# Turning one normalised copy of the tokens instead of two in an attention and feed-forward block

## The reference

```python
xn = _layernorm(x, axis=-1)
x = x + attn(xn, norm_w, Wq, Wkv, Wo, q_gamma, k_gamma) + ffn(xn, W1, b1, W2, b2, scale)
# in attn:
h = xn * rsqrt(mean(xn**2) + eps) * norm_w            # RMS norm over the layer norm
q, k, v = h @ Wq, split(h @ Wkv, 2)                   # 16 heads of 64
q = q / max(norm(q), 1e-12) * (q_gamma + 1) * 8       # each head of each token; k likewise
sim = tanh(q @ k.T / 50) * 50 / 8
out = softmax(sim) @ v @ Wo
```

## Time and profile before

| | |
|---|---|
| median of 3 runs | 1115.67 us (1115.66 to 1117.9) |
| the profiled execution | 1117.53 us |
| its span, first to last instruction | 1115.5 us |
| mean granted TensorE clock | 0.995 |
| busy: PE, PEld, DVE, ACT, POOL | 94%, 75%, 84%, 93%, 77% |
| chain that ended last | PE 49%, ACT 23%, DVE 18%, issue 8%, POOL 0% |
| DMA | 77 GB/s mean |

### The profile page before, as it was taken

How to read it: one execution, slowest core, us unless ns; L and a number is a source line. 1 busy time by engine, 2 the same in 40 slices (tenths; PEclk the granted TensorE clock), 3 DMA queues, 4 the chain that set the end, 5 groups by cost and what they waited for, 6 DMA issues and landing times.

```text
span 1115.5 us, 33883 instructions
## 1 busy us (share of the span) xinstructions
PE 1045.9 (94%) x12873; PEld 835.4 (75%) x12873; DVE 931.7 (84%) x2185; ACT 1034.0 (93%) x1543; POOL 854.0 (77%) x784
## 2 busy tenths in 40 slices
PE   3789999999999999999999999999999999999987
PEld 2557787777787777787777777777778777778776
DVE  4888898888898888889888889888889888889872
ACT  3599999999999999999999999999999999999996
POOL 5577787778788878778778778778778778778663
PEclk9899999999999999999999999999999999999999
DMA  4143343354343344443334444444335344344441
GB/s 149 40 82 68 80 85 69 73 87 73 80 81 73 74 82 76 79 80 77 77 74 79 80 80 78 73 77 80 78 79 82 69 77 87 74 79 77 70 91 30
DMA packets 310743, 86.45 MB, mean 77 GB/s; under 512 B 282036, under 2 KB 309816, under 8 KB 310584
## 3 DMA queue, kind: packets, MB, share of 16 engines
q1 hardware_dynamic: 310584, 84.30, 39.8%
HBM read 12.13 MB, written 4.19 MB: 15 GB/s over the span
## 4 chain that ended last, share of the span: by engine, by line
PE 49%; ACT 23%; DVE 18%; issue 8%; POOL 0%; ACTq 0%; POOLq 0%
PE ps_scores L492 11%; ACT probs L582 6%; ACT clamped L575 6%; PE ps_y L542 6%; PE ps_aux L467 6%; DVE qk L770 6%; PE ps_aux L426 5%; PE ps_o L520 4%; ACT L619 4%; DVE norm L685 3%; PE ps_aux L428 3%; PE ps_aux L427 3%; ACT hid L619 3%; PE ps_y L540 3%; PE ps_o L522 3%
## 5 line engine op out<-in xcount | busy, mean ns | idle before, releaser
L937 POOL TENSOR_TENSOR probs_lo<-probs 128x1024 f16<-128x1024 f32 x256 | 485.1, 1895 | 216.3 <-ACT probs L582 214.1
L575 ACT ACTIVATE clamped<-ps_scores 128x1024 f32<-128x1024 f32 x256 | 265.7, 1038 | 34.6 <-PE ps_scores L492 28.8
L582 ACT ACTIVATE probs<-clamped 128x1024 f32<-128x1024 f32 x256 | 273.3, 1067 | 2.2 <-PE ps_o L522 0.7
L520 PEld LDWEIGHTS ps_o<-v_hi,probs 128*128 128x128 bf16 x2048 | 183.9, 98 | 60.6 <-issue 58.1
L520 PE MATMUL ps_o<-v_hi,probs 128*128 128x65 bf16 x2048 | 213.8, 195 | 5.2 <-DVE newton_r L698 1.7
L492 PE MATMUL ps_scores<-heads_T 64*128 64x256 f16 x3072 | 212.8, 271 | 4.3 <-ACT clamped L575 4.2
L426 PE MATMUL ps_aux<-w_hi,xhT_hi 128*128 128x512 f32 x384 | 179.6, 468 | 38.7 <-DVE qk L770 29.1
L521 PE MATMUL ps_o<-v_lo,probs 128*128 128x64 bf16 x2048 | 211.8, 192 | 0.0
L522 PE MATMUL ps_o<-v_hi,probs_lo 128*128 128x65 bf16 x2048 | 211.4, 193 | 0.0
L521 PEld LDWEIGHTS ps_o<-v_lo,probs 128*128 128x128 bf16 x2048 | 187.3, 99 | 0.0
L522 PEld LDWEIGHTS ps_o<-v_hi,probs_lo 128*128 128x128 f16 x2048 | 187.3, 97 | 0.0
(11 more groups left out here) (80 smaller groups left out, 1927.1 us busy)
## 6 DMA issues: line engine op xcount, KB each, us to landing
heads_T<-halves SPq DMA_TRANSPOSE x512, 2.5
x_in<-in_L_attn_tokens_dram SPq DMA_DIRECT2D x32, 128.0 KB, 2.4
x_res<-in_L_attn_tokens_dram SPq DMA_DIRECT2D x32, 128.0 KB, 2.3
out_dram<-y_sb SPq DMA_DIRECT2D x32, 128.0 KB, 2.5
sel_raw<-xn SPq DMA_DIRECT2D x192, 4.0 KB
qk<-in_L_attn_Wkv_dram SPq DMA_DIRECT2D x2, 512.0 KB, 5.3
qk<-in_L_attn_Wq_dram SPq DMA_DIRECT2D x1, 512.0 KB, 3.7
qk<-in_L_ffn_W_dram SPq DMA_DIRECT2D x2, 256.0 KB
```

Of the source, the lines that this page charges most:

```text
L520: pe.matmul(full, hi[:, col], v_hi[:, par, u, h], start=(u == 0), stop=False)
L575: nc.scalar.activation(clamped[:].rearrange("p j n -> p (j n)"), ps_scores[:].rearrange("p j n -> p (j n)"), ACT.Tanh).then_inc(clamp_done, 1)
L582: nc.scalar.activation(probs[:, pair % RING].rearrange("p j n -> p (j n)"), clamped[:].rearrange("p j n -> p (j n)"), ACT.Exp, bias=LIFT, ...
L937: g.tensor_tensor(probs_lo[:, buf].rearrange("p j n -> p (j n)"), probs[:, buf].rearrange("p j n -> p (j n)"), probs[:, buf].rearrange("p ...
```

## The change

Only `xn` is made and turned. `xhT_hi`, `xhT_lo` and `xnT` are now all made from the turned `xn`. The RMS factor (one number per token) is applied where values leave PSUM, in `v_hi` and in `v_lo`; for queries and keys it goes into the floor under the norm, which is now one number per token and tile. The variance sums move from GpSimd to VectorE, which also divides them (`inv_eps`, `var_eps[:, 1]`); GpSimd keeps the power and makes the floor. The core of the diff:

```diff
-                    for t in range(TT):
-                        pe.transpose(bank[:, t * P:(t + 1) * P], xh[:, t], ident[:])
-                    for t in range(TT):
-                        ins = pe.transpose(bank[:, seq + t * P:seq + (t + 1) * P], xn[:, par, t], ident[:])
+                        ins = pe.transpose(bank[:, t * P:(t + 1) * P], xn[:, par, t], ident[:])
...
+                if kind == "v" and k == 0:
+                    act.wait_ge(rstd_made, b + 1)
...
-                    nc.scalar.copy(v_hi[:, par, t, 8 * c:8 * c + 8, 0:DH],
-                                   bank.rearrange("p (h d) -> p h d", d=DH)).then_inc(v_hi_made, 1)
+                    nc.scalar.activation(v_hi[:, par, t, 8 * c:8 * c + 8, 0:DH],
+                                         bank.rearrange("p (h d) -> p h d", d=DH), ACT.Copy,
+                                         scale=rstd[:, b % 4, 1, t:t + 1]).then_inc(v_hi_made, 1)
...
+                dve.wait_ge(meanvar_made, 2 * b + 2)
+                wait(dve, floor_made, b)
+                v.tensor_scalar(var_eps[:, 0], mean_var[:, :, 1], LN_EPS, None, ALU.add).then_inc(vareps_made, 1)
+                v.tensor_scalar(ms_eps[:], mean_var[:, :, 1], 1.0 + RMS_EPS, RMS_EPS * LN_EPS,
+                                ALU.mult, ALU.add).then_inc(vareps_made, 1)
+                dve.wait_ge(vareps_made, 2 * b + 2)
+                v.reciprocal(inv_eps[:], var_eps[:, 0]).then_inc(inveps_made, 1)
+                dve.wait_ge(inveps_made, b + 1)
+                v.tensor_tensor(var_eps[:, 1], ms_eps[:], inv_eps[:], ALU.mult).then_inc(ratio_made, 1)
...
-                    v.tensor_scalar(minus_half_norm2, norm2[:], NORM2_MIN, -0.5, ALU.max, ALU.mult)\
-                        .then_inc(seed_made, 1)
+                    dve.wait_ge(floor_made, b + 1)
+                    half_of = TT * HEADS
+                    for t in range(TT):
+                        part = slice(t * half_of, (t + 1) * half_of)
+                        v.tensor_scalar(minus_half_norm2[:, part], norm2[:, part], norm_floor[:, b % 4, t:t + 1], -0.5,
+                                        ALU.max, ALU.mult).then_inc(seed_made, 1)
...
-                    v.tensor_tensor(v_lo[:, par, t, 8 * c:8 * c + 8], bank.rearrange("p (h d) -> p h d", d=DH),
-                                    v_hi[:, par, t, 8 * c:8 * c + 8, 0:DH], ALU.subtract).then_inc(v_split, 1)
+                    v.scalar_tensor_tensor(v_lo[:, par, t, 8 * c:8 * c + 8], bank.rearrange("p (h d) -> p h d", d=DH),
+                                           rstd[:, b % 4, 1, t:t + 1], v_hi[:, par, t, 8 * c:8 * c + 8, 0:DH],
+                                           ALU.mult, ALU.subtract).then_inc(v_split, 1)
...
-                g.tensor_scalar(var_eps[:, 0], mean_var[:, :, 1], LN_EPS, None, ALU.add).then_inc(vareps_made, 1)
-                g.tensor_scalar(var_eps[:, 1], mean_var[:, :, 1], 1.0 + RMS_EPS, RMS_EPS * LN_EPS,
-                                ALU.mult, ALU.add).then_inc(vareps_made, 1)
-                pool.wait_ge(vareps_made, 2 * b + 2)
+                pool.wait_ge(ratio_made, b + 1)
...
+                g.tensor_scalar(norm_floor[:, b % 4], var_eps[:, 1], NORM2_MIN, None, ALU.mult).then_inc(floor_made, 1)
...
-                g.tensor_tensor(xh[:], x_mid[:], rstd[:, 1].unsqueeze(2).to_broadcast([P, TT, P]), ALU.mult)\
```

More of the change, by code:

```diff
@@ L194, in block_kernel @@
         var_eps = sb("var_eps", [P, 2, TT])
-        rstd = sb("rstd", [P, 2, TT])
+        ms_eps = sb("ms_eps", [P, TT])
+        inv_eps = sb("inv_eps", [P, TT])
+        rstd = sb("rstd", [P, 4, 2, TT])
+        norm_floor = sb("norm_floor", [P, 4, TT])
         xn = sb("xn", [P, 2, TT, P])
-        xh = sb("xh", [P, TT, P])
         x_mid = sb("x_mid", [P, TT, P])
@@ L267, in block_kernel @@
         seed_made = sem("seed_made")
+        ratio_made = sem("ratio_made")
+        inveps_made = sem("inveps_made")
+        floor_made = sem("floor_made")
         newton_step = sem("newton_step")
@@ L507, in values @@
                 if s == 3:
-                    wait(pe, seed_made, min(2 * (n + 2), 2 * batches))
+                    wait(pe, seed_made, min(3 * (n + 2), 3 * batches))
                 if s in (4, 5):
@@ L595, in aux @@
                 act.wait_ge(aux_filled[kind], PER_BATCH[kind] * b + k + 1)
+                if kind == "v" and k == 0:
+                    act.wait_ge(rstd_made, b + 1)
                 if kind == "xT":
                     nc.scalar.copy(xhT_hi[:, par], bank[:, 0:seq])
-                    nc.scalar.copy(xnT[:, b % 3], bank[:, seq:2 * seq]).then_inc(xnT_copied, 1)
+                    nc.scalar.copy(xnT[:, b % 3], bank[:, 0:seq]).then_inc(xnT_copied, 1)
                 elif kind == "q":
@@ L693, in seed @@
                     wait(dve, newton_step, 9 * b)
-                    v.tensor_scalar(minus_half_norm2, norm2[:], NORM2_MIN, -0.5, ALU.max, ALU.mult)\
-                        .then_inc(seed_made, 1)
+                    dve.wait_ge(floor_made, b + 1)
[4 more added lines that the diff above has]
+                                        ALU.max, ALU.mult).then_inc(seed_made, 1)
                 else:
-                    dve.wait_ge(seed_made, 2 * b + 1)
+                    dve.wait_ge(seed_made, 3 * b + 2)
                     v.tensor_scalar(newton_r[:].bitcast(I32), minus_half_norm2.bitcast(I32), -0.5, RSQRT_SEED,
@@ L704, in newton @@
                 if k == 0:
-                    dve.wait_ge(seed_made, 2 * b + 2)
+                    dve.wait_ge(seed_made, 3 * b + 3)
                 wait(dve, newton_step, 9 * b + k)
@@ L772, in aux @@
                 elif kind == "v":
+                    if k == 0:
+                        dve.wait_ge(rstd_made, b + 1)
                     dve.wait_ge(v_hi_made, 4 * b + k + 1)
                     t, c = k // 2, k % 2
-                    v.tensor_tensor(v_lo[:, par, t, 8 * c:8 * c + 8], bank.rearrange("p (h d) -> p h d", d=DH),
-                                    v_hi[:, par, t, 8 * c:8 * c + 8, 0:DH], ALU.subtract).then_inc(v_split, 1)
+                    v.scalar_tensor_tensor(v_lo[:, par, t, 8 * c:8 * c + 8], bank.rearrange("p (h d) -> p h d", d=DH),
+                                           rstd[:, b % 4, 1, t:t + 1], v_hi[:, par, t, 8 * c:8 * c + 8, 0:DH],
+                                           ALU.mult, ALU.subtract).then_inc(v_split, 1)
                 elif kind == "low":
@@ L856, in norm_rstd @@
                 b, _, _ = st.batch(ahead)
-                pool.wait_ge(meanvar_made, 2 * b + 2)
-                wait(pool, rstd_made, b)
-                g.tensor_scalar(var_eps[:, 0], mean_var[:, :, 1], LN_EPS, None, ALU.add).then_inc(vareps_made, 1)
-                g.tensor_scalar(var_eps[:, 1], mean_var[:, :, 1], 1.0 + RMS_EPS, RMS_EPS * LN_EPS,
-                                ALU.mult, ALU.add).then_inc(vareps_made, 1)
-                pool.wait_ge(vareps_made, 2 * b + 2)
+                pool.wait_ge(ratio_made, b + 1)
                 wait(pool, xn_made, b)
-                g.tensor_tensor(rstd[:].rearrange("p a b -> p (a b)"), var_eps[:].rearrange("p a b -> p (a b)"),
+                wait(pool, v_split, 4 * (b - 3))
+                g.tensor_tensor(rstd[:, b % 4].rearrange("p a b -> p (a b)"), var_eps[:].rearrange("p a b -> p (a b)"),
                                 minus_half[:], ALU.pow).then_inc(rstd_made, 1)
+                wait(pool, seed_made, 3 * (b - 3))
+                g.tensor_scalar(norm_floor[:, b % 4], var_eps[:, 1], NORM2_MIN, None, ALU.mult).then_inc(floor_made, 1)
             def norm_apply(st, ahead):
@@ L874, in norm_apply @@
                 pool.wait_ge(mid_made, b + 1)
-                g.tensor_tensor(xn[:, par], x_mid[:], rstd[:, 0].unsqueeze(2).to_broadcast([P, TT, P]), ALU.mult)
-                g.tensor_tensor(xh[:], x_mid[:], rstd[:, 1].unsqueeze(2).to_broadcast([P, TT, P]), ALU.mult)\
+                g.tensor_tensor(xn[:, par], x_mid[:], rstd[:, b % 4, 0].unsqueeze(2).to_broadcast([P, TT, P]), ALU.mult)\
                     .then_inc(xn_made, 1)
```

## The result

| | before | after |
|---|---|---|
| median | 1115.66 us (1115.57 to 1117.9, 4 runs) | 1130.78 us (1129.7 to 1133.22, 4 runs) |
| ratio, 95% interval | | 1.0134 (1.0111 to 1.0156) |
| profiled execution; its span | 1117.53; 1115.5 us | 1131.7; 1129.4 us |
| mean granted clock | 0.995 | 0.994 |

The change makes the kernel slower by 1.3%, 15 us by the medians, 14 by the profiled executions; forecast were 13.5, a time of 1129 in a range of 1122 to 1134.

What follows compares the result with a forecast made beforehand. The prediction took a loop through TensorE, ScalarE and VectorE, 33.22 us a round, as the bound; v_hi 0.20, v_lo 0.06 and seed 0.19 make 0.45, times 30 is 13.5 us, so 1129 us, range 1122 to 1134.

Steps and rivals of the forecast that it cites:

- v_hi, 0.20 a round: ScalarE, before the copy of k0: the per-partition scale adds 0.10 us each to v0 and v1; v2, v3 left out.
- Rival B: The pointer operand costs nothing on ScalarE, leaving 0.25 us a round, 7.5 us, 1123 us; chance 0.11.
- rival D: More is on the loop, all four v_hi or VectorE's new wait chain: 1135 us and over; chance 0.07.
- v_lo, 0.06: VectorE, step 7: the scalar operand adds 0.06 us each, but only v3's counts, 0.06 a round.
- The seed, 0.19: VectorE's branch before step 3's rounding: two floor operations and their wait take 0.46 for 0.27, 0.19 us a round.
- The turns, nothing: TensorE, step 1: two turns fewer save some 0.22 us a round, but VectorE's later branch covers it, gain nothing.
- Rival A: TensorE's branch with the turns ends the round, added operations are cover: faster, 1109 us; chance 0.04.
- rival C: The change costs nothing that counts, its small prices sit in gaps: same time, 1116 us; chance 0.08.
- Four small operations, nothing: VectorE, step 4: at most 0.94 us, within 1.74 us of idle time there, so no cost.
- The sum: Over the round: 0.20 + 0.06 + 0.19 = 0.45 us, times 30: 13.5 us.
- Tanh's wait for TensorE in step 3: ScalarE's tanh waits 0.19 us for TensorE; the wait was to be smaller or gone.
- Head and tail: Outside the steady rounds: up to 1 us gained from xh, first round pays about the same; together 0, give or take 1.

Runs made afterwards that it cites:

- e1: The changed kernel with v_hi copied without the RMS factor: 1126.06 us, ratio 1.0087.
- e3: The changed kernel with v_lo as a plain subtraction of v_hi from the unscaled values: 1129.62 us, ratio 1.0114.
- e2: The changed kernel with the norm's floor as one operation of 64 columns and a constant, without the RMS factor: 1126.3 us, ratio 1.0093.
- e4: The kernel before with xh neither made nor turned, xhT from the turned xn, RMS factor left out: 1116.98 us, ratio 1.0001.
- e5: The kernel before with the two turns of xh made twice, same output: 1120.89 us, ratio 1.0036.
- e10: The kernel before with the edits of e4 and e9 together: 1111.52 us, ratio 0.995.
- e9: The kernel before with floor, first guess and Newton's first step moved behind step 3's normalise, TensorE's seed wait there removed: 1113.54 us, ratio 0.9973.
- e6: The kernel before with VectorE's second addition of weights (low, 1) moved from step 2 to step 3, behind normalise: 1121.82 us, ratio 1.0048.
- e8: The changed kernel with the floor as one 64-column operation taking norm_floor as a broadcast second tensor: 1161.64 us, ratio 1.0407.
- e7: The changed kernel with VectorE's (low, 1) moved from step 2 to step 3, behind normalise: 1167.68 us, ratio 1.0459.

## Why the prediction was right

The sign, the size and the three terms came out of one claim: the round is a loop through three engines, and what counts is what lies on it.

- **v_hi, 0.20 a round.** 702 ns where 0.70 was forecast, 0.57 apart as forecast; 0.16 between the rounding and k0, and 0.17 by e1. Rival B (the operand costs nothing on ScalarE) falls with the 99 ns. That v2 and v3 don't count is shown by e1's 0.17 against 0.40; with it the case of all four v_hi in rival D falls. The Trainium skill's 93 ns for a pointer operand (ScalarE: Activation LUTs, What ACT_TABLE_LOAD costs) agrees with the 99 ns of the rows.
- **v_lo, 0.06.** 745 ns and 0.07 in the trace, 0.065 by e3, from one of four; in e3 the plain form took 684 ns.
- **The seed, 0.19.** 0.44 from the first floor operation to the first guess (forecast 0.46), 0.18 on the branch. By e2 it is only 0.11; 0.06 of the 0.07 that are missing is the later start of e2's floor operation. Why that starts later stays open. TensorE's new wait for the first guess, 0.4 a round, cost nothing that shows, as forecast: the next division of VectorE, at 601.98, doesn't wait for TensorE, and the one behind it waits 1.07 in after as in before.
- **The turns, nothing.** e4 shows it with nothing else added, e5 that the reserve is 0.09, e10 against e9 that they count once VectorE's branch is shorter, with half of their 0.22. Rival A (TensorE's branch decides) falls, and rival C (nothing counts) with the round of 33.63.
- **Four small operations, nothing.** The first query block's wait went from 1.74 in the earlier trace rows to 1.07, by 0.67, about as forecast:

```profile
575.30 0.17 DVE L678 TENSOR_SCALAR var_eps<-mean_var 128x2 f32<-128x2 f32 x1
...
575.78 0.16 DVE L684 TENSOR_TENSOR var_eps<-ms_eps,inv_eps 128x2 f32<-128x2 f32 x1
577.01 0.69 DVE L789 TENSOR_TENSOR qk<-ps_aux,g_bc 128x512 f32<-128x512 f32 x1 [1.07 <-ACT sq_q L606]
```

**The sum** was 0.45 x 30 = 13.5, and the profiled executions differ by 14.2. That is closer than its parts: the rounds cost 12.5, 1.0 less than forecast, and head and tail 1.4 more, so that 1.0 of the agreement is luck.

Two steps were off.

*Tanh's wait for TensorE in step 3* was to become smaller or go; it is 0.19 as before. The step that failed took that wait as the whole of what TensorE's branch would save. From the start of VectorE's stretch to that tanh it was 592.68 - 586.26 = 6.42 and is 600.65 - 594.36 = 6.29. So the branch got shorter by 0.13 of 0.22, and it did so before that wait. The rest went back behind the turns. TensorE in step 1 of before, then TensorE and ScalarE in step 1 of after:

```profile
586.75 0.61 PE L540 MATMUL ps_y<-w_eff,hid 128*128 128x128 f32 x4
587.19 0.60 PE L467 MATMUL ps_aux<-ident,o_sb 128*128 128x128 f32 x4
587.63 0.61 PE L540 MATMUL ps_y<-w_eff,hid 128*128 128x128 f32 x4
```

```profile
594.62 0.61 PE L543 MATMUL ps_y<-w_eff,hid 128*128 128x128 f32 x4
595.11 0.66 PE L470 MATMUL ps_aux<-ident,o_sb 128*128 128x128 f32 x4
595.60 0.61 PE L543 MATMUL ps_y<-w_eff,hid 128*128 128x128 f32 x4
```

```profile
594.48 0.58 ACT L620 COPY oT<-ps_aux 128x512 f32<-128x512 f32 x1
```

Before, the turns of o start 0.44 after y and take 0.44 to the next; now it is 0.49 and 0.49, together 0.10 more. They start 0.05 after ScalarE's copy of `oT` has ended (594.48 + 0.58 = 595.06), as in e10. With the turns of xh gone, TensorE comes to a bank that ScalarE has not read yet, by these rows and the wait in the code.

*Head and tail* were to come to 0, give or take 1, and cost 1.4 in these two executions. The step that failed is the gain of up to 1 us from xh. The 1.06 of the earlier trace rows did go from GpSimd, but the gammas of VectorE, which wait for GpSimd's masks, start no earlier than the 16.83 of the earlier trace rows:

```profile
16.96 1.23 DVE L811 TENSOR_SCALAR hid<-hid 128x2048 f32<-128x2048 f32 x1 [2.66 <-POOL mask L939]
```

Two of GpSimd's masks took 1.69 and 1.41 us where they had taken 0.72 and 0.63, and VectorE's three `w_lo`, beside which they run, 4.51 in place of 3.57. e4 confirms that nothing is gained: xh is gone there and nothing is added, and its gammas start at 16.81 and its 30 rounds begin at 60.85, where those of before begin at 60.84.

What the 1.20 up to the start of the 30 rounds is made of stays open. The gammas have 0.13 of it, and the first guess of the first batch comes at 36.10 instead of 35.69. The other 0.79 arise in the first round, in which VectorE pays the small operations, the seed and v, but in which TensorE's granted clock differs too: from 44 to 48 us it was 0.83 before and is 0.50, the lower of its two levels (1.2 GHz), in after; from 52 to 56 us it was 0.57 and is 1.00. Nor is one execution's head a firm measure: in e2 the first guess comes at 34.15, 1.95 before that of after, though its edit touches nothing earlier. TensorE's matmuls of 512 columns follow each other there every 0.23 us from 28 on, in after every 0.43 until 31.5.

## What to carry to other kernels

In a loop through several engines, look at each handover for which branch comes last and by how much. A saving on the other branch is worth nothing, a cost on it only what exceeds the reserve (0.13 of 0.22 in e5), and a saving starts to count once the later branch is shortened (nothing in e4, 0.11 from e9 to e10). Before an operation is moved on an in-order engine, ask who waits for it and what is queued behind that wait: two moves out of the same branch gave +5 us (e6) and -3 us (e9). And if a factor is moved from one cheap operation to the place where results leave PSUM, it is paid once per tile there, on engines that may be on the loop.

## What was not expected of the hardware

An operation of VectorE of 64 columns with two inputs in SBUF took between 233 and 1684 ns, by where it fell on a GpSimd instruction (e8), and even one of two columns with a single input, from SBUF to SBUF, took 1.64 us in place of 0.17 in such a place (e7). So a small operation that costs 0.2 us in one order of the work may cost 1.6 in another. On ScalarE the per-partition scale costs 99 ns in an instruction's length and 0.10 in the distance to the next. On VectorE v_lo with it takes 60 ns more (745 against 685), though there the kind of instruction changes as well. The floor kept its kind: it took 228 ns with a constant and 64 columns, and 249 with the scalar and only 32.
